# Two layers of cross attention with feed-forward: key loads, residual loads and a bias addition at other places in their queues

## The chip, the cores and the metric

One NeuronCore of one Trainium2 chip. Times are device microseconds of one execution of the whole program. One execution was also taken by the hardware profiler; all rows below are from it. TensorE (PE) does the matrix products, VectorE (DVE), ScalarE (ACT) and GpSimd (POOL) the rest; SyncE (SP) issues almost all DMA transfers, in one queue and in program order (SPq in the rows).

## The reference, cut to what matters

```
x: (32, 256, 256), context: (32, 77, 192), 16 heads of 64
x = x + attention0(layernorm(x), context)       # Wq, Wk, Wv, Wo, bo; softmax over 77 keys
x = x + down(silu(gate(n)) * up(n))             # n = layernorm(x); 256 -> 768 -> 256, int weights / 127
x = x + attention1(layernorm(x), context)       # same shapes, other weights
x = x + dequantised(int8(n) @ int8(rhs))        # n = layernorm(x); row and column scales absmax / 127
```

## The kernel before, in words

A first stage turns the context into keys and values of both layers, as high and low 16-bit halves, and stores them in DRAM. The main stage runs 64 batches: `h` = 0 to 31 are the 32 batches of layer 0, `h` = 32 to 63 those of layer 1. Each engine has its own `body(h, like, lay, plan)`, and the order of its work in it is written out by hand. `lay[d]` is the layer (0, 1 or None) of the batch `h + d`; work of up to seven neighbouring batches is interleaved in one body. The bodies of `h` = 4 to 28 and 36 to 60 run as hardware loops, the others are unrolled (line 815).

A body has four slots, `u` = 0 to 3, one for each unit of four heads. In slot `u`:

- TensorE computes the scores of unit `u` of batch `h` in two halves of 128 queries (line 960), queries of a unit two further on (970), the output projection of unit `u` of batch `h-1` (983) and the weighting of values three units back (998). Feed-forward products of batches `h-2` and `h-3` (1006, 1013), or the quantised product (1019), stand in between.
- VectorE takes the row maxima of the scores (1291), forms low halves (1217, 1220) and reciprocals of the denominators (1296); ScalarE computes the exponentials (1140). In slot 3 VectorE sums the projection and the residual rows `x_res` to `x1` (1399). In slot 0 of the next body follow its moments (1231, 1233).
- GpSimd makes the probabilities of a half of a unit in three operations: multiplication by the reciprocals (1436), high half (1440), low half (1442). In slot `u` it does the second half of unit `u-1`, then the first half of unit `u`. At the end of slot 3 it takes the power for the normalisation (1415, tile `rs`). At the end of slot 0 it adds the output bias to the residual rows (1465).
- SyncE turns the probabilities by a transposing DMA, one for each half of unit `u-1` in slot `u` (849, tile `pT`). The buffer `p16` exists twice: GpSimd's high half of a unit waits until the unit two before has been turned. Around the turnings stand the other transfers: residual rows in slot 0 (897), keys of units 2 and 3 in slot 0 and of units 0 and 1 of the next batch in slot 2 (833, two DMAs each, tile `kb`), values in slots 1 and 3 (840), normalised rows of layer 1 in slot 2 (907), results (913, 919, 930).

The keys of units 2 and 3 are read from slot 2 on; those of units 0 and 1, loaded in slot 2, from slot 0 of the next body. A key buffer may be overwritten once the scores that read it are done (semaphore `s_s`). The normalised rows of the next but one batch are turned by TensorE in slot 1 of the next body. The bias waits for the residual load (`s_xr`); line 1399 waits for the bias (`s_xb`).

Of the kernel before, what the change touches and what calls it, by code (L numbers as in the profile page):

```python
# [50 lines left out]
def xattn_ffn_kernel(nc, x, ctx, wq0, wk0, wv0, wo0, bo0, w_gate, w_up, w_down,  # L51
                     wq1, wk1, wv1, wo1, bo1, rhs, out):
    B, NQ, D = x.shape
# [3 lines left out]
    QT = NQ // P  # L57
# [19 lines left out]
    with stack:  # L77
# [29 lines left out]
        x_in, xn = (x_pair[:, i, :].rearrange("p (t d) -> p t d", d=D) for i in range(2))  # L107
        st1 = sb("st1", [P, QT, 6], F32)
        mv1 = sb("mv1", [P, QT, 2], F32)
        ve1 = sb("ve1", [P, QT], F32)  # L110
        rs1 = sb("rs1", [P, QT], F32)
# [535 lines left out]
        x_res = sb("x_res", [P, QT, D], F32)  # L647
# [52 lines left out]
        s_xr, s_xb, s_x1 = sem("s_xr"), sem("s_xb"), sem("s_x1")  # L700
        s_nl, s_ngo, s_ygo = sem("s_nl"), sem("s_ngo"), sem("s_ygo")
# [30 lines left out]
        def batch_of(ap, b):  # L732
            return ap[bass.ds(b, 1)].rearrange("o p t d -> (o p) t d")

        def after(eng, s, count):

            if not (isinstance(count, int) and count <= 0):
                eng.wait_ge(s, count)
# [88 lines left out]
        with nc.Block() as block:  # L827

            @block.sync
            def _(sp):  # L830
                def load_keys(g, at, l):
                    for a in range(2):
                        sp.dma_start(kb[g][a * DH:(a + 1) * DH, :, :, a * NK:(a + 1) * NK].rearrange(  # L833
                            "p r m k -> p (r m) k"),
                            keys_d[l][a * DH:(a + 1) * DH, g, :, bass.ds(at, NK)]).then_inc(s_kb[g], 16)

                def load_values(g, at, l):
                    src = vals_d[l].rearrange("r k c -> k r c")[bass.ds(at, NK), :,
                                                               g * 2 * HPU * DH:(g + 1) * 2 * HPU * DH]
                    sp.dma_start(vb[g][:, :, :], src).then_inc(s_vb[g], 16)  # L840

                def turn_probabilities(k, v, t):

                    if t == 0:
                        after(sp, s_pv, k - 3)
                        sp.sem_inc(s_pgo, 1)
                    sp.wait_ge(s_pl, QT * k + t + 1)
                    sp.sem_inc(s_pgo, 1)
                    sp.dma_start_transpose(pT[v][:, :, t * P:(t + 1) * P],  # L849
                                           p16[v % 2][:, t, :, :, :].rearrange("p r h k -> p (r h k)")).then_inc(  # L850
                                               s_pt[v], 16)

                def ready(e):

                    return e if isinstance(e, int) else sp.snap(e)

                def load_late():
                    for k, item in enumerate(late_items):
                        d, src = late_raw[:, k, :], item[0]
                        if len(src.shape) == 3:  # L860
                            d = d.rearrange("p (t d) -> p t d", d=D)
                        sp.dma_start(d, src).then_inc(s_late, 16)

                sp.sem_inc(s_y, 16)
                sp.sem_inc(s_ys, 16)
                sp.wait_ge(s_xn, QT)
                sp.dma_start(x_in[:, :, :], batch_of(x_src[0], 1)).then_inc(s_x, 16)
                sp.wait_ge(s_kz, 4)
                load_keys(0, 0, 0)
                load_keys(1, 0, 0)  # L870
                sp.wait_ge(s_xn, QT * 2)
                sp.dma_start(x_in[:, :, :], batch_of(x_src[0], 2)).then_inc(s_x, 16)

                def body(h, like, lay, plan):
                    n = UNITS * h
                    if lay[-3] == 0:
                        b_mid = ready(h - 3)
                    if lay[-2] == 1:
                        b_out = ready(h - 2 - B)
                    if lay[-1] is not None:  # L880
                        b_res = ready(h - 1 - lay[-1] * B)
                    if lay[0] is not None:
                        at_own = ready((h - lay[0] * B) * NK)
                    if lay[1] is not None:
                        at_next = ready((h + 1 - lay[1] * B) * NK)
                    if lay[2] == 1:
                        b_far = ready(h + 2 - B)
                    if lay[3] == 0:
                        b_first = ready(h + 3)
                    for u in range(UNITS):  # L890
                        turning = lay[(u - 1) // UNITS] is not None
                        if u == 0 and lay[-1] is not None:
                            after(sp, s_x1, h - 1)
                            if lay[-1] == 1:
                                sp.sem_inc(s_ngo, 1)
                                sp.wait_ge(s_y, 16 * (h - 1 - B + 2))
                            sp.dma_start(x_res[:, :, :], batch_of(x_src[lay[-1]], b_res)).then_inc(s_xr, 16)
                        if turning:
                            turn_probabilities(n + u - 1, (u - 1) % UNITS, 0)
                        if u == 1 and lay[0] is not None:  # L900
                            after(sp, s_pv, n - 2)
                            load_values(0, at_own, lay[0])
                        if u == 2 and lay[2] == 1:
                            sp.wait_ge(s_ys, 16 * (h + 4 - B))
                            sp.sem_inc(s_ngo, 1)
                            sp.wait_ge(s_xt, h + 2)
                            sp.dma_start(xn, batch_of(n_rows, b_far)).then_inc(s_nl, 16)
                        if u == 2 and lay[1] is not None:
                            sp.wait_ge(s_s, QT * (n + 2))
                            load_keys(0, at_next, lay[1])  # L910
                        if u == 3 and lay[-2] == 1:
                            sp.wait_ge(s_ysum, h - 1 - B)
                            sp.dma_start(batch_of(out_rows, b_out), yo[:, :, :]).then_inc(s_yo, 16)
                        if u == 3 and lay[0] is not None:
                            after(sp, s_pv, n)
                            load_values(1, at_own, lay[0])
                        if u == 3 and lay[-3] == 0:
                            sp.wait_ge(s_yn, QT * (h - 2))
                            sp.dma_start(batch_of(n_rows, b_mid), yn[:, :, :]).then_inc(s_ys, 16)
                        if turning:  # L920
                            turn_probabilities(n + u - 1, (u - 1) % UNITS, 1)
                        if u == 3 and lay[3] == 0:
                            sp.wait_ge(s_xn, QT * (h + 3))
                            sp.dma_start(x_in[:, :, :], batch_of(x_src[0], b_first)).then_inc(s_x, 16)
                        if u == 0 and lay[0] is not None and like > 0:
                            sp.wait_ge(s_s, QT * n)
                            load_keys(1, at_own, lay[0])
                        if u == 2 and lay[-3] == 0:
                            sp.wait_ge(s_yd, QT * (h - 2))
                            sp.dma_start(batch_of(mid_rows, b_mid), y[:, :, :]).then_inc(s_y, 16)  # L930
                        if like == 0 and u == 3:
                            load_late()

                bodies(sp, body)
                sp.wait_ge(s_y, 16 * (B + 1))
                sp.wait_ge(s_ys, 16 * (B + 1))
                sp.wait_ge(s_yo, 16 * B)
# [474 lines left out]
            def _(pool):  # L1412
                def inverse(k, ve, rs, count):
                    pool.wait_ge(s_var[k], count)
                    pool.tensor_tensor(rs[:, :], ve[:, :], half_neg[:, :], ALU.pow).then_inc(s_inv[k], 1)  # L1415
# [7 lines left out]
                def body(h, like, lay, plan):  # L1423
# [21 lines left out]
                    for u in range(UNITS):  # L1445
# [13 lines left out]
                            pool.tensor_copy(y[:, :, :], x1[:, :, :]).then_inc(s_yx, 1)  # L1459
                        if lay[0] is not None:  # L1460
                            probabilities(h, u, 0)
                        if u == 0 and lay[-1] is not None:
                            pool.wait_ge(s_xr, 16 * h)
                            bias = bo_b[lay[-1]][:, :].unsqueeze(1).to_broadcast([P, QT, D])
                            pool.tensor_tensor(x_res[:, :, :], x_res[:, :, :], bias, ALU.add).then_inc(s_xb, 1)
                        if u == 1 and lay[2] == 0:
                            inverse(0, ve1, rs1, h + 2)
                        if u == 2 and lay[-2] == 0:
                            low_hidden(0, h - 2)
                        if u == 2 and lay[-3] == 0:  # L1470
# [32 lines left out]
```

## Time and profile before

| | |
|---|---|
| median of 3 runs | 1768.03 us |
| all runs | 1763.06, 1768.2, 1768.03 us |
| the profiled execution | 1763.16 us, its span 1761.4 us |
| granted TensorE clock, mean | 0.988 |
| busy share of the span | PE 93%, ACT 78%, DVE 77%, POOL 72% |
| hardware DMA queue | 282.87 MB, 74.0% of the 16 DMA engines' time |

The page gives the busy share of every engine over the whole span. The stages differ, so the rows below are taken from stretches of it: layer 0 runs to about 1070 us, the turnover to about 1170, layer 1 from there to about 1730. In a row of the timeline the columns are the start, the time busy, engine, line, operation, what it writes and reads, and in brackets the idle time before it and what ended it. In the waits the columns are the total in us, the number of waits and the longest.

### The profile page before, as it was taken

How to read it: one execution, taken by the hardware profiler on the slowest of the kernel's cores; microseconds unless marked ns; L12 is line 12 of the kernel's file. 1: busy time of each engine (PE TensorE's matmuls, PEld its weight loads, DVE VectorE, ACT ScalarE, POOL GpSimd, SP SyncE). 2: the span in 40 equal slices, each digit the busy share in tenths (PEclk: the TensorE clock that was granted, in tenths of full speed). 3: DMA queues.
4: the chain of work that ended last, by engine and by line, in shares of the span. 5: the costliest groups of instructions: out<-in, count | busy, mean ns of one | idle time of the engine just before them, and what ended most of it. 6: DMA issues, size and time to landing. Idle time of an engine off the chain costs nothing.

```text
span 1761.4 us, 56617 instructions
## 1 busy us (share of the span) xinstructions
PE 1646.6 (93%) x16300; PEld 1399.7 (79%) x16300; DVE 1359.9 (77%) x3471; ACT 1373.6 (78%) x5650; POOL 1268.4 (72%) x1920
## 2 busy tenths in 40 slices
PE   7999858999999999999999999999989999899995
PEld 6888746888888888888888888877777777777773
DVE  5666646888888888888888887787777777777775
ACT  5555548888888888888888887788888888888883
POOL 3000157878888888887888887888888888888883
PEclk9999989999999999999999999999999999999998
DMA  8666757776666667666666677798888888888894
GB/s 234 223 227 221 253 140 152 138 149 144 139 147 147 136 148 149 135 149 149 136 148 151 129 148 154 133 186 175 174 174 174 173 177 177 171 174 173 178 177 85
DMA packets 807766, 288.45 MB, mean 164 GB/s; under 512 B 686000, under 2 KB 795472, under 8 KB 807696
## 3 DMA queue, kind: packets, MB, share of 16 engines
q1 hardware_dynamic: 806432, 282.87, 74.0%
q0 software_dynamic: 1264, 4.72, 0.9%
q8 instruction: 35, 0.57, 0.1%
q14 instruction: 35, 0.29, 0.1%
HBM read 87.72 MB, written 65.54 MB: 87 GB/s over the span
## 4 chain that ended last, share of the span: by engine, by line
PE 55%; SPq 8%; POOL 8%; issue 7%; DMA 3%; DVE 3%; ACT 1%; POOLq 0%; ACTq 0%; DVEq 0%
PE psum L970 12%; PE psum L983 12%; PE psum L1006 9%; PE psum L960 8%; PE psum L998 7%; SPq L849 5%; PE psum L1013 5%; POOL pr L1436 3%; DMA kb<-keys 3%; POOL p L1442 2%; POOL p L1440 2%; PE psum L946 2%; SPq L833 2%; DVE oT_l L1217 1%; ACT ex L1140 1%
## 5 line engine op out<-in xcount | busy, mean ns | idle before, releaser
L1140 ACT ACTIVATE ex<-psum,nmax 128x77 f32<-128x77 f32 x2048 | 635.5, 331 | 70.1 <-DVE nmax L1291 66.2
L1140 ACT ACTIVATION_READ_ACCUMULATOR ex<-psum,nmax 128x1 f32 x2048 | 434.7, 212 | 0.0
L1442 POOL TENSOR_TENSOR p<-pr,p 128x308 f16<-128x308 f32 x512 | 393.9, 769 | 40.9
L1436 POOL TENSOR_TENSOR pr<-ex,rden 128x308 f32<-128x308 f32 x512 | 358.8, 701 | 43.3 <-DVE rden L1296 39.8
L1291 DVE TENSOR_REDUCE nmax<-psum 128x4 f32<-128x308 f32 x512 | 240.1, 469 | 169.7 <-PE psum L960 166.1
L1440 POOL CAST p<-pr 128x308 f16<-128x308 f32 x512 | 231.4, 452 | 106.1 <-POOL pr L1436 102.6
L983 PE MATMUL psum<-wo_h,oT_h 128*128 128x256 f16 x1024 | 281.1, 275 | 24.2 <-DVE oT_l L1217 23.7
L960 PE MATMUL psum<-kb,qT_h 128*128 128x154 f16 x2048 | 257.8, 231 | 48.1 <-DMA kb<-keys 34.9
L970 PE MATMUL psum<-xT_h,wq_h 128*128 128x256 f16 x1024 | 281.1, 274 | 1.4 <-DVE xT_l L1217 1.4
L970 PE MATMUL psum<-xT_l,wq_h 128*128 128x256 f16 x1024 | 281.2, 275 | 0.0
L970 PE MATMUL psum<-xT_h,wq_l 128*128 128x256 f16 x1024 | 281.0, 274 | 0.0
L983 PE MATMUL psum<-wo_l,oT_h 128*128 128x256 f16 x1024 | 280.9, 274 | 0.0
L983 PE MATMUL psum<-wo_h,oT_l 128*128 128x256 f16 x1024 | 280.9, 274 | 0.0
L960 PEld LDWEIGHTS psum<-kb,qT_h 128*128 128x128 f16 x2048 | 167.1, 98 | 103.5 <-ACT ex L1140 45.4
L960 PE MATMUL psum<-kb,qT_l 128*128 128x154 f16 x1024 | 221.4, 230 | 0.0
L998 PE MATMUL psum<-pT,vb 77*64 77x256 f16 x3072 | 217.4, 277 | 0.0
L1102 ACT ACTIVATE oT_h<-psum 128x512 f16<-128x512 f32 x256 | 154.7, 604 | 60.8 <-PE psum L998 60.6
L998 PEld LDWEIGHTS psum<-pT,vb 77*64 77x64 f16 x3072 | 148.4, 110 | 54.6 <-issue 54.3
L1217 DVE TENSOR_TENSOR oT_l<-psum,oT_h 128x512 f16<-128x512 f32 x256 | 174.9, 683 | 14.4 <-ACT oT_h L1102 14.2
L1220 DVE SCALAR_TENSOR_TENSOR qT_l<-psum,qT_h 128x512 f16<-128x512 f32 x256 | 173.9, 679 | 0.2 <-ACT qT_h L1102 0.2
L1102 ACT ACTIVATE qT_h<-psum 128x512 f16<-128x512 f32 x256 | 156.0, 610 | 3.6 <-PE psum L970 3.6
L1415 POOL TENSOR_TENSOR rs<-ve,half_neg 128x2 f32<-128x2 f32 x127 | 88.6, 697 | 73.1 <-DVE ve L1233 70.1
(161 smaller groups left out, 3855.3 us busy)
## 6 DMA issues: line engine op xcount, KB each, us to landing
keys<-ks SPq DMA_DIRECT2D x14, 1408.0 KB, 6.3
kb<-keys SPq DMA_DIRECT2D x256, 77.0 KB, 3.2
vb<-vals SPq DMA_DIRECT2D x128, 154.0 KB
vals<-vs SPq DMA_DIRECT2D x56, 256.0 KB, 2.5
x_pair<-in_x_dram SPq DMA_DIRECT2D x32, 256.0 KB, 2.8
pT<-p SPq DMA_TRANSPOSE x512, 3.2
x_res<-in_x_dram SPq DMA_DIRECT2D x32, 256.0 KB, 3.3
mid_x<-y SPq DMA_DIRECT2D x32, 256.0 KB, 2.5
```

What stands on the lines that cost most here:

```text
L960: last = pe.matmul(o, w[:, a, ts], kb[u // 2][:, part, u % 2 * PPU + a, :], start=(q == 0), stop=(q == 2))
L970: last = pe.matmul(o[:, a, :], ww[:, k, w], xx[:, k, :], start=(q == 0), stop=(q == len(terms) - 1))
L983: last = pe.matmul(OA[:, t, :], oo[:, a, ts], ww[:, m, :], start=first, stop=(u == UNITS - 1 and a == PPU - 1 and q == 2), skip_group_chec ...
L998: last = pe.matmul(OV[b * DH:(b + 1) * DH, a, :], vb[u // 2][:, part, c:c + DH], pT[u][0:NK, pp * HPU + hd, :], start=(q == 0), stop=(q == 2))
L1102: return act.activation(dst, src, ACT.Copy, scale=scale)
L1140: last = act.activation(ex[i][:, t, b, :], SC[:, t, b * NK:(b + 1) * NK], ACT.Exp, bias=nmax[i][:, t, b:b + 1], accum_out=den[i][:, t, b:b ...
L1217: return dve.tensor_tensor(dst, src, hi, ALU.subtract)
L1220: return dve.scalar_tensor_tensor(out=qT_l[i][:, :, :], in0=src, scalar=Q_DOWN, in1=qT_h[i][:, :, :], op0=ALU.mult, op1=ALU.subtract)
L1291: dve.tensor_reduce(nmax[i][:, t, :], SC[:, t, :].rearrange("p (h k) -> p h k", k=NK), AX_X, ALU.max, negate=True).then_inc(s_m, 1)
L1436: pool.tensor_tensor(pr[:, t, :, :], ex[i][:, t, :, :], r, ALU.mult).then_inc(s_p, 1)
L1440: pool.tensor_copy(d[:, t, 0, :, 0:NK], pr[:, t, :, :]).then_inc(s_ph, 1)
L1442: pool.tensor_tensor(d[:, t, 1, :, 0:NK], pr[:, t, :, :], d[:, t, 0, :, 0:NK], ALU.subtract).then_inc(s_pl, 1)
```

## The change

On SyncE, the key loads come first in slots 0 and 2, with the same semaphore waits. The residual load (slot 0) and the load of the normalised rows (slot 2) come after both turnings of their slot. On GpSimd, the bias addition goes from the end of slot 0 to the end of slot 1, behind the power operation `inverse(0, ...)` of layer 0. No instruction is added or taken away.

```diff
                     for u in range(UNITS):
                         turning = lay[(u - 1) // UNITS] is not None
-                        if u == 0 and lay[-1] is not None:
-                            after(sp, s_x1, h - 1)
-                            if lay[-1] == 1:
-                                sp.sem_inc(s_ngo, 1)
-                                sp.wait_ge(s_y, 16 * (h - 1 - B + 2))
-                            sp.dma_start(x_res[:, :, :], batch_of(x_src[lay[-1]], b_res)).then_inc(s_xr, 16)
+                        if u == 0 and lay[0] is not None and like > 0:
+                            sp.wait_ge(s_s, QT * n)
+                            load_keys(1, at_own, lay[0])
+                        if u == 2 and lay[1] is not None:
+                            sp.wait_ge(s_s, QT * (n + 2))
+                            load_keys(0, at_next, lay[1])
                         if turning:
                             turn_probabilities(n + u - 1, (u - 1) % UNITS, 0)
...
-                        if u == 2 and lay[2] == 1:
-                            sp.wait_ge(s_ys, 16 * (h + 4 - B))
-                            sp.sem_inc(s_ngo, 1)
-                            sp.wait_ge(s_xt, h + 2)
-                            sp.dma_start(xn, batch_of(n_rows, b_far)).then_inc(s_nl, 16)
-                        if u == 2 and lay[1] is not None:
-                            sp.wait_ge(s_s, QT * (n + 2))
-                            load_keys(0, at_next, lay[1])
...
                         if turning:
                             turn_probabilities(n + u - 1, (u - 1) % UNITS, 1)
+                        if u == 0 and lay[-1] is not None:
+                            after(sp, s_x1, h - 1)
+                            if lay[-1] == 1:
+                                sp.sem_inc(s_ngo, 1)
+                                sp.wait_ge(s_y, 16 * (h - 1 - B + 2))
+                            sp.dma_start(x_res[:, :, :], batch_of(x_src[lay[-1]], b_res)).then_inc(s_xr, 16)
+                        if u == 2 and lay[2] == 1:
+                            sp.wait_ge(s_ys, 16 * (h + 4 - B))
+                            sp.sem_inc(s_ngo, 1)
+                            sp.wait_ge(s_xt, h + 2)
+                            sp.dma_start(xn, batch_of(n_rows, b_far)).then_inc(s_nl, 16)
...
-                        if u == 0 and lay[0] is not None and like > 0:
-                            sp.wait_ge(s_s, QT * n)
-                            load_keys(1, at_own, lay[0])
...
-                        if u == 0 and lay[-1] is not None:
+                        if u == 1 and lay[2] == 0:
+                            inverse(0, ve1, rs1, h + 2)
+                        if u == 1 and lay[-1] is not None:
                             pool.wait_ge(s_xr, 16 * h)
                             bias = bo_b[lay[-1]][:, :].unsqueeze(1).to_broadcast([P, QT, D])
                             pool.tensor_tensor(x_res[:, :, :], x_res[:, :, :], bias, ALU.add).then_inc(s_xb, 1)
-                        if u == 1 and lay[2] == 0:
-                            inverse(0, ve1, rs1, h + 2)
```

## Rows read from the trace of the kernel before

**Rows 1.** Busy time by stretch; first column the stretch, second its length.
```profile
core 0: us, PE busy (x) PEld busy (x) DVE busy (x) ACT busy (x) POOL busy (x), PEclk, DMA share, GB/s
1190.51:1653.69 463.18, 426.31 (x4686) 358.27 (x4683) 355.60 (x922) 390.61 (x1772) 397.13 (x598) 1.00 0.86 175
355.00:994.00 639.00, 637.43 (x6641) 548.18 (x6638) 552.34 (x1487) 537.70 (x2243) 521.22 (x803) 1.00 0.68 145
...
1096.66:1123.56 26.90, 26.00 (x276) 22.52 (x273) 20.14 (x56) 21.18 (x91) 20.89 (x32) 1.00 0.82 142
```

**Rows 2.** Waits of TensorE, GpSimd and SyncE, 1320 to 1640 us.
```profile
PE psum L960 <- DMA kb<-keys: 20.3, 15, 1.6
...
POOL pr L1436 <- DVE rden L1296: 5.7, 23, 0.3
POOL p L1440 <- DMA pT<-p: 1.5, 6, 0.3
...
SPq L848 <- POOL p L1442: 9.9, 21, 0.6
```

**Rows 3.** Groups of instructions, same stretch: busy us, mean ns | idle before.
```profile
L1415 POOL TENSOR_TENSOR rs<-ve,half_neg 128x2 f32<-128x2 f32 x16 | 11.2, 699 | 1.6
```

**Rows 4.** The chain that ended last, 1380 to 1440 us: start, us, what.
```profile
1416.46 3.10 DMA kb<-keys
```

**Rows 5.** Timeline of SyncE, one batch of layer 1.
```profile
1405.46 2.79 SPq L849 DMA_TRANSPOSE pT<-p  x2
...
1411.81 0.40 SPq L897 DMA_DIRECT2D x_res<-mid_x  x1
1412.57 2.71 SPq L849 DMA_TRANSPOSE pT<-p  x2
1415.56 1.51 SPq L833 DMA_DIRECT2D kb<-keys  x2
```

**Rows 6.** Timeline of TensorE, slot 2 of the same batch.
```profile
1419.79 0.30 PE L960 MATMUL psum<-kb,qT_h 128*128 128x154 f16 x2 [1.50 <-DMA kb<-keys]
```

**Rows 7.** DMA issues, 1391 to 1431 us; last column us to landing.
```profile
x_res<-mid_x SPq DMA_DIRECT2D x2, 256.0 KB, 2.8
```

**Rows 8.** Timeline of GpSimd, same batch.
```profile
1410.49 0.70 POOL L1415 TENSOR_TENSOR rs<-ve,half_neg 128x2 f32<-128x2 f32 x1
...
1412.73 0.75 POOL L1442 TENSOR_TENSOR p<-pr,p 128x308 f16<-128x308 f32 x1
...
1414.85 1.04 POOL L1442 TENSOR_TENSOR p<-pr,p 128x308 f16<-128x308 f32 x1
1415.86 1.26 POOL L1465 TENSOR_TENSOR x_res<-x_res,bo_b 128x512 f32<-128x512 f32 x1
1417.09 0.69 POOL L1436 TENSOR_TENSOR pr<-ex,rden 128x308 f32<-128x308 f32 x1
...
1421.64 0.70 POOL L1436 TENSOR_TENSOR pr<-ex,rden 128x308 f32<-128x308 f32 x1 [0.27 <-DVE rden L1296]
```

**Rows 9.** Timeline of VectorE, same batch.
```profile
1414.85 0.43 DVE L1331 TENSOR_SCALAR q_i<-q_a 128x512 f16<-128x512 f32 x1 [0.51 <-ACT q_a L1197]
...
1415.85 0.17 DVE L1296 RECIPROCAL rden<-den 128x4 f32<-128x4 f32 x1
...
1421.39 0.17 DVE L1296 RECIPROCAL rden<-den 128x4 f32<-128x4 f32 x1
```

**Rows 10.** The bias additions, whole span: ns min/median/max.
```profile
L1465 POOL TENSOR_TENSOR x_res<-x_res,bo_b x64: 1257/1272/1534, 268.0 to 1734.7; 128x512 f32<-128x512 f32 x64
```

**Rows 11.** Timeline of TensorE, two batches of the turnover.
```profile
1081.53 0.29 PE L960 MATMUL psum<-kb,qT_h 128*128 128x154 f16 x2 [0.92 <-issue]
...
1108.43 0.29 PE L960 MATMUL psum<-kb,qT_h 128*128 128x154 f16 x2 [0.90 <-issue]
```

**Rows 12.** DMA issues, 1076 to 1077.6 us; last column us to landing.
```profile
kb<-keys SPq DMA_DIRECT2D x2, 77.0 KB, 3.9
```

**Rows 13.** Timelines of GpSimd and VectorE, a late batch.
```profile
1692.78 0.70 POOL L1415 TENSOR_TENSOR rs<-ve,half_neg 128x2 f32<-128x2 f32 x1
...
1699.11 0.70 POOL L1436 TENSOR_TENSOR pr<-ex,rden 128x308 f32<-128x308 f32 x1
...
1698.56 0.17 DVE L1296 RECIPROCAL rden<-den 128x4 f32<-128x4 f32 x1
```

**Rows 14.** Timeline of GpSimd, one batch of layer 0.
```profile
705.00 0.69 POOL L1415 TENSOR_TENSOR rs<-ve,half_neg 128x2 f32<-128x2 f32 x1 [1.80 <-DVE ve L1233]
```

## The prediction

> **What bounds the kernel now.** I read the busy time by stage first, because the batches of the two layers are different work [rows 1]. In layer 0 TensorE is busy 637.43 of 639.00 us: nothing outside it can show in the time there. In layer 1, from 1190.51 to 1653.69 us, it is busy 426.31 of 463.18. The residual loads, one a batch, divide that stretch into 23 batches of 20.14 us; TensorE works 18.5 of them and is idle 1.6. So only layer 1 and the few batches around the turnover can answer.
>
> Second, the waits of layer 1, over 320 us or 15.9 batches [rows 2]. TensorE waits 20.3 us for key loads, 1.28 a batch, the wait that the change is about. GpSimd, only fourth in busy time on the page, waits for almost nothing: 5.7 us for reciprocals (0.36 a batch) and 1.5 us for turned probabilities (0.09), and 1.6 us stand idle ahead of its power operation (0.10) [rows 3]. Everything else in its 20.14 us is its own work and the fixed gaps between its dependent operations. The DMA-issuing queue, SyncE, waits 9.9 us for probabilities (0.62 a batch): it too is nearly full. Third, the chain of waits goes from SyncE through a key load's landing [rows 4] into TensorE's scores, on through the residual sum and its moments to GpSimd, and from GpSimd's probabilities back to SyncE. The key load is on that loop; GpSimd and SyncE are right behind it. That limits the gain: if TensorE's 1.28 us went, the batch would shrink by no more than GpSimd's own slack, 0.36 + 0.09 + 0.10 = 0.55 us.
>
> **Keys of units 2 and 3, to the head of slot 0.** Now SyncE issues in slot 0 the residual load at 1411.81, both turnings from 1412.57, and the keys from 1415.56 [rows 5]. The second half lands 3.10 us after 1416.46 [rows 4], at 1419.56, and TensorE goes on at 1419.79 after 1.50 us of idleness [rows 6]. With the keys in the place of the residual load they are issued 3.75 us earlier and land at about 1415.8. TensorE wants them at 1419.79 - 1.50 = 1418.3: 2.5 us of cover, so the wait goes. Their semaphore condition, all scores of the batch before, holds long before, since GpSimd's last probabilities, for which the turnings wait, come after those scores. What becomes late is the rest of the slot. The two key issues take 1.51 us, the residual load's place was 0.76 (1412.57 - 1411.81), so the turnings shift by 0.75 us at worst, if SyncE is then still as far behind as now. I expect them unshifted, because of the next edit.
>
> **Keys of units 0 and 1, to the head of slot 2.** Now the normalised rows and then these keys stand between the two turnings of the slot, and the second turning, at 1405.46 [rows 5], is the one whose landing GpSimd waits for [rows 2]. The keys are read a whole pair of slots later, so they gain nothing themselves. But ahead of the turnings they fill the time in which SyncE waits for GpSimd, and the second turning stands behind nothing. Gain: the 0.09 us a batch, and a SyncE that comes to slot 0 on time.
>
> **Normalised rows, behind the turnings of slot 2.** Read by TensorE in slot 1 of the next batch, three slots later; nothing is lost. **Residual load, behind the turnings of slot 0.** The turnings end their issue at 1412.57 + 2.71 = 1415.28 [rows 5], at worst 0.75 later, and the load lands 2.8 us after its issue [rows 7], so at 1418.2 to 1419.0. Its reader is the bias.
>
> **The bias, one slot later on GpSimd.** This is the part that costs. Count from the power operation at 1410.49 [rows 8]. GpSimd reaches the second half of unit 0's probabilities (the multiplication by the reciprocals, at 1417.09) 6.60 us after it, with the bias in between. Start to start the bias takes 1417.09 - 1415.86 = 1.23 us; without it GpSimd would be there after 5.37 us. But the reciprocals that this step reads are made by VectorE at 1415.85 and end at 1416.02 [rows 9], which is 5.53 us after the same power operation, and a GpSimd step follows a reciprocal by 0.08 us (1421.39 + 0.17 = 1421.56, start at 1421.64) [rows 8, 9]. The 5.53 us are a chain: power, shift, normalisation on ScalarE, row maximum, scale, the rounding for the quantised product (1414.85, VectorE waiting 0.51 us for ScalarE [rows 9]), low half of the output, reciprocal. None of it waits for keys, so it does not shorten when they come early. GpSimd would stand 5.61 - 5.37 = 0.24 us in each batch. Before, the bias covered exactly this. The later place costs nothing else. Two steps take (1421.64 - 0.27 - 1417.09) = 4.28 us [rows 8], so the bias starts 5.61 + 4.28 = 9.9 us after the power operation, at 1420.4, at least 1.4 us after its load has landed; its result is read in slot 3. It also stands ahead of the step that now waits 0.27 us for reciprocals at 1421.64, and those come earlier once the scores of unit 2 do, so the 0.36 us goes.
>
> The bias could gain or lose in length. It takes 1257 to 1534 ns, median 1272 [rows 10], so the bounds are -0.01 and +0.26 us; I take 0, by the median. The Trainium skill (SBUF — State Buffer, Who interferes with whom) says that a VectorE operation with two SBUF inputs, or in a two-port mode, and a GpSimd operation that reads SBUF exclude each other. The trace agrees: the subtraction beside the rounding at 1414.85 took 1.04 us, the others 0.75 [rows 8, 9]. By that rule the moved bias would pay only if it met such an operation; the VectorE work beside 1420.4 is a maximum and a difference that reads PSUM.
>
> **Sum for layer 1.** Gone: 0.36 + 0.09. Added: 0.24. The 0.10 ahead of the power operation goes if VectorE comes earlier with TensorE; bounds 0 and 0.10. That is 0.21 to 0.31 us a batch; I take 0.25, a batch of 19.89. Twenty-five batches run in this form (the 23 of rows 1 and one at either side): 25 x 0.25 = 6.3 us.
>
> **Turnover.** Two batches in which TensorE still does layer 0's FFN are bound by TensorE (26.00 of 26.90 us busy [rows 1]), and it stands some 0.9 us in each, just ahead of unit 2's scores [rows 11]. The profile names no releaser there, but those keys took 3.9 us to land [rows 12] in place of 3.1. I count these as key waits: 1.8 us, bounds 0 and 1.8.
>
> **Tail.** In the last batches the same count gives GpSimd 1699.11 - 1692.78 = 6.33 us with the bias, 5.10 without its 1.23, against reciprocals 1698.56 + 0.17 - 1692.78 = 5.95 us after the power operation [rows 13]. GpSimd waits for nothing there now, so the change can only lose: 0 to 0.9 us in each of two batches. I take 0.4 each, -0.8.
>
> **Layer 0.** Cost nothing. TensorE covers all: GpSimd there waits 1.80 us for VectorE once a batch [rows 14], more than the bias is long. If that cover were gone, 26 batches at 0.24 would be 6 us. The start I leave at nothing, within the 1.3 us of one bias.
>
> Sum: 6.3 + 1.8 - 0.8 = 7.3 us. The profiled execution took 1763.16 us (span 1761.4), so it would become 1755.9. The median of the runs, 1768.03, lies 4.87 above the profiled one, since two of three runs are near 1768: 1760.7, rounded to **1760**.
>
> **Rivals.**
> (a) GpSimd never waits: the chain behind the power operation is hidden after all, because VectorE and ScalarE run ahead once keys are early. Then each batch gains 0.55: 25 x 0.55 + 1.8 - 0.8 = 14.8 us, 1753. For it: GpSimd's pure work is the floor. Against: the chain starts on GpSimd itself, so running ahead does not help.
> (b) The wait is replaced in full: SyncE (0.62 us of slack) or ScalarE's exponentials hold TensorE as long as the keys did, or the keys are no earlier because SyncE comes late to the slot. Only the turnover gains, 1 to 2 us: 1766. For it: GpSimd and SyncE are within a microsecond of the period. Against: 3.75 us of lead is 2.5 times the wait.
> (c) Slower: the residual load is late. The bias wants it at 1420.4, with 1.4 to 2.2 us in hand; the load stands behind two turnings, on DMA engines that are 86% busy in this stage [rows 1]. It decides once the landing takes over 4.2 us (median 2.8), if the turnings are shifted. At 5.1 us GpSimd, which has no slack left, stands 0.9 us a batch: 25 x (0.9 - 0.25) = 16 us, less the turnover's 1: 1783. For it: key loads took 3.9 us in the turnover [rows 12]. Against: in the steady stage the load takes two thirds of that.
>
> **How the numbers follow.** Forecast 50%, (a) 20%, (b) 20%, (c) 8%, the rest 2%. The forecast's own range is 1756 to 1764: terms of 0.21 to 0.31 a batch, 0 to 1.8, 0 to -1.8, and 2.5 us for which of the two times of the runs the median falls on. With (a) in and most of (b): 1750 to 1767. A difference under 0.3%, 5.3 us, can't be told from none. Faster (under 1762.7): most of the forecast and all of (a), 0.71. Same: most of (b) and the upper end of the forecast, 0.22. Slower: 0.07.
>
> **What would show it.** Right: TensorE has no wait for keys in layer 1; the batch is 19.8 to 20.0 us; GpSimd waits some 0.2 us for reciprocals in every batch, now ahead of the second half of unit 0 and no more in slots 2 and 3; none for turned probabilities; layer 0 stays at 26.2 us. Wrong: a batch of 19.6 (rival a) or 20.1 (b), or a GpSimd wait for the residual load (c).

## The result, and the profile after

| | before | after |
|---|---|---|
| median of 12 runs each | 1768.12 us | 1774.1 us |
| lowest to highest | 1761.77 to 1772.81 | 1771.85 to 1782.97 |
| profiled execution, span | 1763.16, 1761.4 us | 1771.97, 1770.2 us |

The ratio is 1.0042, 95% interval 1.0027 to 1.0058. The change made the kernel slower, where 1760 us was forecast.

One sum per batch, VectorE's `x1` (line 1399), divides both traces in the same way. The start of each of those operations gives this ledger:

| stretch | before | after | difference |
|---|---|---|---|
| start of the span to batch 1 | 281.97 | 285.25 | +3.28 |
| batches 2 to 28 (layer 0) | 709.13 | 704.86 | -4.27 |
| batches 29 to 35 (turnover) | 174.76 | 172.24 | -2.52 |
| batches 36 to 60 (layer 1) | 504.11 | 514.03 | +9.92 |
| batches 61 to 64 | 78.57 | 80.97 | +2.40 |

The first row is not put down to the change. The context stage runs without the edited code, and 2.33 of the 3.28 us are there already at the first row maximum of the main stage (236.97 us before, 239.30 after). The first `x1` lay between 285.29 and 288.56 us in every other profiled execution below, with the bias and the keys in either place. Without this row, 5.5 of the 8.8 us between the two profiled executions are left; the medians differ by 6.0. In the settled part a layer 0 batch went from 26.22 to 26.09 us, one of layer 1 from 20.14 to 20.57.

The stretches of the kernel after that answer to [rows 1] (stretch, length, busy time by engine, clock, DMA share, GB/s):

```profile
1182.79:1676.38 493.59, 453.69 (x4898) 373.61 (x4898) 382.96 (x960) 402.22 (x1849) 409.05 (x625) 1.00 0.84 171
355.00:994.00 639.00, 637.40 (x6666) 550.74 (x6664) 536.25 (x1495) 537.15 (x2255) 519.22 (x808) 1.00 0.67 145
```

The waits of the kernel after, 1320 to 1640 us, 15.6 batches, for [rows 2]:

```profile
PE psum L960 <- DVE qT_l L1220: 14.9, 15, 1.0
...
POOL pr L1436 <- DVE rden L1296: 18.4, 15, 1.2
...
SPq L848 <- POOL p L1442: 16.7, 16, 1.1
...
DVE nmr L1238 <- POOL rs L1415: 23.3, 16, 1.5
```

TensorE's wait for keys is gone, as is GpSimd's for turned probabilities, and SyncE, which had 0.62 us of slack a batch, now has 1.07. All that the change set out to do on SyncE it did. GpSimd's wait for reciprocals has grown from 5.7 to 18.4 us. It is now one wait a batch of 1.22 us, at the place that the prediction named, where 0.24 us was forecast. These are GpSimd and VectorE of one batch after, for [rows 8, 9]:

```profile
1433.54 0.70 POOL L1415 TENSOR_TENSOR rs<-ve,half_neg 128x2 f32<-128x2 f32 x1
1434.19 0.71 POOL L1436 TENSOR_TENSOR pr<-ex,rden 128x308 f32<-128x308 f32 x1
...
1439.77 0.70 POOL L1436 TENSOR_TENSOR pr<-ex,rden 128x308 f32<-128x308 f32 x1 [1.23 <-DVE rden L1296]
```
```profile
1434.27 0.65 DVE L1238 SCALAR_TENSOR_TENSOR nmr<-mv,rs 128x2 f32<-128x2 f32 x1 [1.45 <-POOL rs L1415]
...
1438.45 0.43 DVE L1331 TENSOR_SCALAR q_i<-q_a 128x512 f16<-128x512 f32 x1 [0.72 <-ACT q_a L1197]
1438.83 0.69 DVE L1217 TENSOR_TENSOR oT_l<-psum,oT_h 128x512 f16<-128x512 f32 x1
1439.44 0.17 DVE L1296 RECIPROCAL rden<-den 128x4 f32<-128x4 f32 x1
```

The chain from the power operation at 1433.54 to the step at 1439.77 takes 6.23 us; 5.61 were forecast from [rows 8, 9]. The new part stands at its head. The shift (`nmr`, two numbers a partition) takes 0.65 us. It starts 0.08 us after GpSimd has begun to multiply, and ends within 0.02 us of that multiplication. In the trace of before it took 0.16 (with the reciprocals that the multiplication reads):

```profile
1410.92 0.16 DVE L1296 RECIPROCAL rden<-den 128x4 f32<-128x4 f32 x1
1411.22 0.16 DVE L1238 SCALAR_TENSOR_TENSOR nmr<-mv,rs 128x2 f32<-128x2 f32 x1
```

It started there 0.73 us after the power operation, as it does now (1434.27 - 1433.54). But GpSimd's multiplication came 0.78 us after that operation, and now comes 0.65 after it. The reciprocals that it reads ended 0.59 us after the start of the power operation; now they end 0.73 us ahead of it, and the multiplication starts before the shift. The order was a matter of 0.1 us already in the kernel before. In its batches with power operations at 1672.58 and 1692.78 the multiplication started 0.67 us after the power operation, and the shift took 0.66 us:

```profile
1673.31 0.66 DVE L1238 SCALAR_TENSOR_TENSOR nmr<-mv,rs 128x2 f32<-128x2 f32 x1
```

What put the multiplication at 0.78 us in the other batches, with reciprocals that ended at 0.59 us in both, is not shown.

The chain is 0.62 us longer than forecast, and the shift makes 0.49 of that. The rest is two small pieces: VectorE's scale (line 1284) takes 0.30 us where it took 0.24, and GpSimd starts 0.16 us behind the end of the reciprocals, not 0.08. GpSimd's own way to that step became shorter, 5.01 us where 5.37 was forecast: its multiplication starts 0.1 us sooner, and its low half (1442) takes 0.75 us in place of 1.04, now that VectorE's rounding starts only near its end. So 0.24 us became 0.24 + 0.62 + 0.36 = 1.22. The last term lengthens the wait and not the batch.

The chain of waits of the kernel after, same view as [rows 4], runs through exactly these steps and no more through SyncE or a key load (start, us, what; three pieces named "issue" left out behind the shift and the row maximum):

```profile
1433.54 0.71 POOL rs L1415
1434.27 0.06 DVE nmr L1238
...
1434.84 0.48 DVE nmax L1291
...
1435.46 0.59 ACT x L1106
1436.08 0.70 DVE am L1379
...
1438.45 0.44 DVE q_i L1331
...
1439.77 0.71 POOL pr L1436
```

### The profile page after: what moved, and what is told of

It reads as the page before. It is cut to its first block, busy times and chain, and to the rows that moved or that the text cites. A ratio compares the mean times of both kernels' runs of the same rounds, so it can differ in the third digit from the quotient of the medians.

```text
span 1770.2 us, 56617 instructions
## 1 busy us (share of the span) xinstructions
PE 1652.9 (93%) x16300; PEld 1400.5 (79%) x16300; DVE 1351.7 (76%) x3471; ACT 1364.7 (77%) x5650; POOL 1254.7 (71%) x1920
## 4 chain that ended last, share of the span: by engine, by line
PE 46%; POOL 19%; issue 11%; DVE 5%; ACT 3%; DMA 1%; POOLq 1%; SPq 0%; ACTq 0%; DVEq 0%
PE psum L970 9%; PE psum L1006 9%; PE psum L983 9%; POOL pr L1436 7%; PE psum L960 6%; PE psum L998 5%; POOL p L1440 5%; PE psum L1013 5%; POOL p L1442 2%; POOL x_res L1467 2%; PE psum L946 2%; POOL rs L1415 1%; DVE am L1379 1%; ACT q_a L1197 1%; ACT x L1106 1%
## 5 line engine op out<-in xcount | busy, mean ns | idle before, releaser
L1140 ACT ACTIVATION_READ_ACCUMULATOR ex<-psum,nmax 128x1 f32 x2048 | 457.4, 223 | 0.0
L983 PEld LDWEIGHTS psum<-wo_h,oT_h 128*128 128x128 f16 x1024 | 100.3, 98 | 53.4 <-DVE oT_l L1217 37.2
```

The costliest lines, as they stand in the source:

```text
L983: last = pe.matmul(OA[:, t, :], oo[:, a, ts], ww[:, m, :], start=first, stop=(u == UNITS - 1 and a == PPU - 1 and q == 2), skip_group_chec ...
L1140: last = act.activation(ex[i][:, t, b, :], SC[:, t, b * NK:(b + 1) * NK], ACT.Exp, bias=nmax[i][:, t, b:b + 1], accum_out=den[i][:, t, b:b ...
```

## The experiments

The first four ran in one set (before: 1771.06 us, median of 24 runs), the last three in another (1770.33, 11 runs). The changed kernel was not timed again in them, so what is said against it goes by the ratios to before and by the batch lengths in the traces. Theory A in all: the loss comes from the bias leaving the place where it covered the chain behind the power operation, and the key order by itself is a gain.

**Keys alone.** The bias stays at the end of slot 0, so the residual load stays first.

```diff
 # the changed kernel, with
+ (SyncE, slot 0) residual load ahead of load_keys(1, ...), no more behind the turnings
- (GpSimd) if u == 1 and lay[-1] is not None: bias
+ (GpSimd) if u == 0 and lay[-1] is not None: bias
```

> Keys first in slots 0 and 2 as in the change, but the bias stays at the end of slot 0, so the residual load stays first in slot 0 (the keys right behind it). Theory A (the loss comes from the bias leaving its place, where it covered the chain from GpSimd's power operation to the reciprocals of unit 0's second half): GpSimd needs 5.01 + 1.23 us from the power operation to that step, the chain 6.23, so no wait; a layer 1 batch of 19.35 to 19.5 us, against 20.14 before and 20.57 after. Layer 0 stays at 26.22. In all about 1749 us where before is 1768. Rival B (the new order on SyncE or on the DMA engines is what costs, by later turnings): batch 20.4 or more, 1772 or more, the wait of some 1.2 us at that step still there.

Measured: 1751.83 us, ratio 0.9897 (0.9869 to 0.9924). A layer 1 batch takes 19.70 us, one of layer 0 26.22. GpSimd waits for nobody in layer 1; its only listed idle time is the fixed gap ahead of its own cast:

```profile
POOL p L1440 <- POOL pr L1436: 27.0, 130, 0.3
```

Rival B is out. The batch is 0.2 to 0.35 us longer than I expected. GpSimd's own operations are longer here, 1502 ns for the bias and 761 for a multiplication, where the changed kernel has 1268 and 699; its low halves are a little shorter, 754 ns against 792 (groups of instructions, keys-only kernel):

```profile
L1436 POOL TENSOR_TENSOR pr<-ex,rden 128x308 f32<-128x308 f32 x131 | 99.7, 761 | 0.0
...
L1465 POOL TENSOR_TENSOR x_res<-x_res,bo_b 128x512 f32<-128x512 f32 x16 | 24.0, 1502 | 0.0
```

The shift takes 0.65 us here too, so the lengthened chain is there, and covered. The bias stands over its end:

```profile
1407.20 0.70 POOL L1415 TENSOR_TENSOR rs<-ve,half_neg 128x2 f32<-128x2 f32 x1
...
1412.18 1.50 POOL L1465 TENSOR_TENSOR x_res<-x_res,bo_b 128x512 f32<-128x512 f32 x1
1413.63 0.70 POOL L1436 TENSOR_TENSOR pr<-ex,rden 128x308 f32<-128x308 f32 x1
```
```profile
1413.12 0.17 DVE L1296 RECIPROCAL rden<-den 128x4 f32<-128x4 f32 x1
```

The reciprocals end at 1413.29, while GpSimd is still adding.

**Bias alone.**

```diff
 # the kernel before, with
-                        if u == 0 and lay[-1] is not None:
-                            (bias)
                         if u == 1 and lay[2] == 0:
                             inverse(0, ve1, rs1, h + 2)
+                        if u == 1 and lay[-1] is not None:
+                            (bias)
```

> Only the bias moves to the end of slot 1; SyncE's order is that of before. Theory A: the key wait of TensorE stays, GpSimd gets a wait of 0.24 us or more at the second half of unit 0; batch 20.14 to 20.3. Layer 0 goes to 26.09, because GpSimd's low half of the hidden rows in slot 1 no longer stands behind the bias and the down product stops waiting 0.13 us: 28 x 0.13 = 3.6 us gained. In all 1764 to 1769. Rival B: the bias is harmless, batch 20.14, 1764, layer 0 as said. Rival C (layer 0's 0.13 us comes from the key order): layer 0 at 26.22.

Measured: 1781.75 us, ratio 1.0065 (1.004 to 1.0091). Layer 0 came out as expected, 26.09. Layer 1 did not: 20.56 to 20.88 a batch, not 20.14 to 20.3. Its waits, 1320 to 1640 us:

```profile
POOL pr L1436 <- DVE rden L1296: 19.6, 16, 1.2
...
PE psum L960 <- DMA kb<-keys: 1.1, 3, 0.4
```

GpSimd waits 1.23 us with the old key order too, and the shift takes 0.65 us. So the longer chain needs no early keys. The keys-only kernel shows that it needs no waiting GpSimd either: there GpSimd waits for nobody, and the shift takes 0.65 us. What all these kernels share is that the reciprocals for the multiplication behind the power operation are ready in time: they end 0.7 us ahead of its start in the changed kernel and in most batches here, 0.1 us ahead with the keys alone, and 0.59 us after it in the kernel before. The key wait of TensorE has all but gone although the keys stand where they stood in SyncE's order. TensorE is held by others now: 15.6 us by VectorE's low halves of the queries (1220) and 5.6 us by exponentials (1140). Why its batches are up to 0.3 us longer than those of the changed kernel was not followed up.

**GpSimd waits for the shift.**

```diff
                         if u == 3 and lay[-1] is not None:
                             inverse(1, ve2, rs2, h)
+                            if lay[-1] == 1:
+                                pool.wait_ge(s_nmr[1], h)
```

> The changed kernel, with one wait more: in layer 1 GpSimd, after the power operation, waits until VectorE has made the shift from it, before it multiplies again. Theory A says that the shift takes 0.65 us in place of 0.16 because GpSimd's multiplication starts 0.08 us before it and both read SBUF through one port: then the shift is back at 0.16, the chain at about 5.75 in place of 6.23, the batch at 14.34 + 5.75 = 20.1, total about 1763. Rival D (the length of the shift is not what lengthens the chain, the wait only delays GpSimd): batch 20.57 or up to 0.3 more, total 1774 to 1781.

Measured: 1766.69 us, ratio 0.9983 (0.9967 to 0.9999), 20.20 a batch. In its trace the 16 shifts of the stretch took (ns min/median/max)

```profile
L1238 DVE SCALAR_TENSOR_TENSOR nmr<-mv,rs x16: 160/161/161, 1329.8 to 1632.8; 128x2 f32<-128x2 f32 x16
```

and in the changed kernel

```profile
L1238 DVE SCALAR_TENSOR_TENSOR nmr<-mv,rs x16: 648/648/648, 1331.4 to 1639.9; 128x2 f32<-128x2 f32 x16
```

One wait more makes the kernel 0.37 us a batch faster. Rival D is out: the 0.49 us is the overlap with GpSimd's multiplication and it does lengthen the batch. The reciprocals of unit 0's second half end 5.46 us after the power operation (1415.16 + 0.17 - 1409.87), in place of 6.07. The wait costs GpSimd 0.72 us a batch in its place, and its own way to unit 0's second half then takes 5.81 us, so that it no longer waits there for the reciprocals (last row, VectorE):

```profile
1409.87 0.70 POOL L1415 TENSOR_TENSOR rs<-ve,half_neg 128x2 f32<-128x2 f32 x1
1411.29 0.70 POOL L1436 TENSOR_TENSOR pr<-ex,rden 128x308 f32<-128x308 f32 x1 [0.72 <-DVE nmr L1238]
...
1415.68 0.70 POOL L1436 TENSOR_TENSOR pr<-ex,rden 128x308 f32<-128x308 f32 x1
```
```profile
1415.16 0.17 DVE L1296 RECIPROCAL rden<-den 128x4 f32<-128x4 f32 x1
```

The Trainium skill (SBUF — State Buffer, Who interferes with whom) has this case: a VectorE instruction with two SBUF inputs contends with a GpSimd instruction that reads SBUF, and issue order decides who blocks. The shift reads `mv` and `rs`, both in SBUF; by that rule it waits for the rest of the multiplication, and the 0.65 us agrees.

**Reciprocals ahead of the rounding.** In layer 1, VectorE makes the reciprocals of unit 0's second half before it rounds for the quantised product.

```diff
+                        if u == 1 and lay[-2] == 1 and lay[0] is not None:
+                            reciprocals(n, 0, 1)
                         if u == 1 and lay[-2] == 1:
                             dve.wait_ge(s_qa, QT * (h - 1 - B))
                             (rounding)
 ...
-                        if lay[(u - 1) // UNITS] is not None:
+                        if lay[(u - 1) // UNITS] is not None and not (u == 1 and lay[-2] == 1):
                             reciprocals(n + u - 1, (u - 1) % 2, 1)
```

> The changed kernel, with VectorE's reciprocals of unit 0's second half moved ahead of the rounding for the quantised product (layer 1 only). Their input is ready when ScalarE has done the exponentials, about 4.3 us after the power operation (3.3 before, 0.5 later by the longer shift, with the reciprocals 0.4 after that), and GpSimd is there after 5.01. Theory A: GpSimd waits no more; batch 14.34 + 5.01 = 19.35, up to 19.6; total about 1747. Rival B (turnings or SyncE hold the batch): batch 20.4 to 20.6, total 1773, GpSimd waiting somewhere else.

Measured: 1768.57 us, ratio 0.9986 (0.9969 to 1.0003), 20.31 a batch. The wait at that step is gone, as expected. The gain, 0.26 us a batch, was about a quarter of what I expected, because the same chain goes on through VectorE to the reciprocals of unit 1's first half, the next that GpSimd needs:

```profile
1413.38 0.70 POOL L1417 TENSOR_TENSOR rs<-ve,half_neg 128x2 f32<-128x2 f32 x1
...
1418.36 0.93 POOL L1438 TENSOR_TENSOR pr<-ex,rden 128x308 f32<-128x308 f32 x1
...
1421.45 0.70 POOL L1438 TENSOR_TENSOR pr<-ex,rden 128x308 f32<-128x308 f32 x1 [0.70 <-DVE rden L1296]
```

It is still GpSimd's wait for VectorE and no turning; rival B is out here too. I had taken the first late operand for the only one. Both lie behind the chain, and a bias at the end of slot 0 covers both.

**Bias by layer.** The keys-only kernel, with the bias at the end of slot 1 where layer 0's rows are added.

```diff
-                        if u == 0 and lay[-1] is not None:
+                        if u == 0 and lay[-1] == 1:
                             (bias)
                         if u == 1 and lay[2] == 0:
                             inverse(0, ve1, rs1, h + 2)
+                        if u == 1 and lay[-1] == 0:
+                            (bias)
```

> The keys-only kernel, with the bias at the end of slot 1 in batches that add layer 0's residual rows and at the end of slot 0 in those of layer 1. Theory A: both gains together: layer 0 at 26.09 us a batch (the down product no longer waits 0.13 us), layer 1 at 19.70. About 28 x 0.13 = 3.6 us below the keys-only kernel's 1751.8: 1748. Rival: the layer 0 gain belongs to the key order and the bias together, or is lost at the turnover: 1752.

Measured: 1749.12 us, ratio 0.988 (0.9862 to 0.9898): 26.09 us a batch in layer 0 and 19.68 to 19.71 in the settled part of layer 1. Its profiled execution is 4.5 us shorter than the keys-only one. Between the medians of the two the difference, 2.7 us, is near what the runs scatter. It has the lowest time of all kernels here.

**Slot 0 keys alone.** The kernel before with `load_keys(1, ...)` moved up behind the residual load, and nothing else.

```diff
                             sp.dma_start(x_res[:, :, :], batch_of(x_src[lay[-1]], b_res)).then_inc(s_xr, 16)
+                        if u == 0 and lay[0] is not None and like > 0:
+                            sp.wait_ge(s_s, QT * n)
+                            load_keys(1, at_own, lay[0])
```

> The kernel before with one edit: the keys of units 2 and 3 go to slot 0 right behind the residual load, ahead of both turnings; the keys of units 0 and 1 and the normalised rows stay between the turnings of slot 2. Theory A (the key wait of TensorE was the outermost of the limits, GpSimd the next): batch 19.7, no key wait, total 1752, perhaps 0.1 us a batch more for GpSimd's wait for turned probabilities, 1754. Rival (the reorder of slot 2 carried the gain, by letting SyncE catch up): batch 20.0 or more, 1763 to 1768.

Measured: 1756.8 us, ratio 0.9925 (0.9908 to 0.9942), 19.71 a batch. The one edit carries the gain of the key order. The edit of slot 2 adds what it was reckoned at, GpSimd's wait for turned probabilities (2.1 us in 320, 0.13 a batch), but in the settled batches this does not show in the length. The two profiled executions are level up to batch 60 (1660.21 and 1660.46 us); 2.9 of the 3.2 us between them arise in the last four. I did not follow these up.

**Bias back, SyncE as changed.** This asks whether the two edits had to go together.

```diff
 # the changed kernel, with
-                        if u == 1 and lay[-1] is not None:
+                        if u == 0 and lay[-1] is not None:
                             (bias)
```

> The changed kernel with SyncE's whole new order, but the bias back at the end of slot 0, so that it follows its load closely. The load would be issued about 4.4 us after the power operation (second turning's probabilities 2.9, issue 1.3, gap 0.2) and land 2.8 to 3.2 later, at 7.2 to 7.6; GpSimd wants it at 5.0. Theory A: GpSimd waits 2.2 to 2.6 us for the residual load in each layer 1 batch; batch 19.7 + 2.4 = 22.1, total 1752 + 28 x 2.4 = about 1815, layer 0 at 26.22 or more. Rival: the load is not late; batch 19.7, 1752.

Measured: 1862.45 us, ratio 1.0529 (1.0509 to 1.055), batches of 21.2 to 25.3 us in layer 1, 23.4 on average.

```profile
1411.10 0.70 POOL L1415 TENSOR_TENSOR rs<-ve,half_neg 128x2 f32<-128x2 f32 x1
...
1420.38 1.27 POOL L1465 TENSOR_TENSOR x_res<-x_res,bo_b 128x512 f32<-128x512 f32 x1 [4.26 <-DMA x_res<-mid_x]
```
```profile
1412.17 1.50 SPq L833 DMA_DIRECT2D kb<-keys  x2
1414.05 2.68 SPq L849 DMA_TRANSPOSE pT<-p  x2
1417.17 0.41 SPq L919 DMA_DIRECT2D x_res<-mid_x  x1
```

Behind the turnings the residual load goes out 6.1 us after the power operation, not 4.4, since the keys push the turnings back, and lands at 9.3. The mechanism was right, the size 4.0 us a batch (55.7 us in 14 waits) in place of 2.4. One thing more differs here: in layer 1 the granted TensorE clock of this kernel was 0.94, where the changed kernel's was 1.00 over the same stretch (the third figure from the end of each row, this kernel first). From 1410 to 1420 us, for one, with TensorE busy for 6.88 us, it was 0.83, so part of that stretch ran at the lower of the two levels, 1.2 and not 2.4 GHz. How much of the length is the clock was not separated.

```profile
1200.00:1700.00 500.00, 425.07 (x4330) 350.66 (x4328) 341.29 (x854) 358.73 (x1640) 364.34 (x554) 0.94 0.73 150
1200.00:1700.00 500.00, 460.03 (x4968) 379.02 (x4966) 388.60 (x976) 408.12 (x1876) 414.91 (x634) 1.00 0.85 171
```

So a residual load behind the turnings forces the bias out of slot 0, and the bias out of slot 0 is the loss. The key loads need neither: the 0.76 us of issue that the residual load takes ahead of them is no burden on keys with 2.5 us of cover.

## Why the prediction was wrong, step by step

- **Keys of units 2 and 3.** Right: the wait is gone in all kernels that issue these keys ahead of the turnings, but for 2.8 us in four waits where the bias went back. Rival (a), the 0.55 us a batch that it can give, is nearly what the keys alone gave: 20.14 to 19.70, 0.44.
- **Keys of units 0 and 1, normalised rows.** Right: they took GpSimd's 0.09 us away and cost nothing.
- **Residual load.** Right in the settled batches: no wait for it there in the changed kernel, and rival (c) did not happen. In the last batch GpSimd did wait for it:

```profile
1748.14 1.26 POOL L1467 TENSOR_TENSOR x_res<-x_res,bo_b 128x512 f32<-128x512 f32 x1 [4.21 <-DMA x_res<-mid_x]
```

  No loss can be seen from it. The last `x1` follows the one before by 21.12 us, and by 21.36 with the keys alone, where nothing waits for that load.
- **The bias: the step that failed.** The place and the mechanism were right, and the term was mis-sized. A batch is GpSimd's way from unit 0's second half round to the power operation, plus the chain from there. The first part was reckoned at 19.89 - 5.61 = 14.28 us and measured 1433.54 - 1419.20 = 14.34. The chain was put at 5.61, carried over from before, and measured 6.23 (14.34 + 6.23 = 20.57, the batch). "So it does not shorten when they come early" was true and not enough: it got longer. 0.49 of the 0.62 us is the shift behind the multiplication; keeping the two apart gave 0.37 us a batch back (third experiment), GpSimd's own way then being the longer. The longer chain stood in the prediction's own rows: in the late batch of [rows 13] the reciprocals end 5.95 us after the power operation, where [rows 8, 9] give 5.53, and the shift of that batch took 0.66 us. I used the 5.95 for the tail and did not ask why it was longer. I weighed the port rule for the moved bias alone, and not for the operations that the new wait shifts against each other. 25 x (0.25 + 0.43) = 17 us is more than the whole miss of 14; layer 0 gave some of it back.
- **Turnover.** Forecast 1.8 us, measured 2.5. The waits there were key waits: they are gone in the changed kernel and with the keys alone, and with the bias alone two of them, 0.57 and 0.93 us, are left. The seven batches take 172.01 us with the keys alone and 174.98 with the bias alone.
- **Tail.** Forecast -0.8, measured -2.4. The cause of layer 1 is at work here too: GpSimd waits 2.4 us for reciprocals in three waits over the last 92 us, 0.7 before, and not at all with the keys alone, which lose 0.2 there. It need not be the only one, since the kernel with slot 0 keys alone loses 3.1 us in these batches and has the bias in its old place. That is open.
- **Layer 0, "cost nothing".** Wrong, for the better: 0.13 us a batch. TensorE was busy without a gap in both, but the first down product of a batch took 1.44 us in the chain of before and 1.31 after:

```profile
714.98 1.44 PE psum L1013 x12
```
```profile
715.41 1.31 PE psum L1013 x12
```

  It comes with the bias (bias alone 26.09, keys alone 26.22). The expectation of the second experiment gave GpSimd's low half of the hidden rows (1426) as the reason, and the trace does not bear that out: in the kernel before it ends at 713.30, 1.62 us ahead of the product's first weight load. What ends 0.12 us ahead of that load is VectorE's low half of the normalised rows (`xT_l`, at 714.80), which frees the bank that the product writes:

```profile
714.11 0.69 DVE L1217 TENSOR_TENSOR xT_l<-psum,xT_h 128x512 f16<-128x512 f32 x1
714.92 0.10 PEld L1013 LDWEIGHTS psum<-wdT,hT_h 128*128 128x128 f16 x1
```

  VectorE was late there because of the bias. Its own low half of the hidden rows, which reads two operands in SBUF, started 0.02 us behind GpSimd's bias addition and took 1.53 us. With the bias elsewhere it took 0.41 (before, before, after):

```profile
711.22 1.27 POOL L1465 TENSOR_TENSOR x_res<-x_res,bo_b 128x512 f32<-128x512 f32 x1
711.24 1.53 DVE L1217 TENSOR_TENSOR hT_l<-hf,hT_h 128x256 f16<-128x256 f32 x1
```
```profile
711.66 0.41 DVE L1217 TENSOR_TENSOR hT_l<-hf,hT_h 128x256 f16<-128x256 f32 x1
```

  It takes 1.53 us also with the keys alone, and 0.41 also with the bias alone and with the bias by layer. So the same kind of overlap that cost the shift 0.49 us in layer 1 was what the moved bias took away in layer 0. A wait of 0.13 us did not show as idle time of TensorE but as a longer first product.
- **The chances.** The forecast counted a loss only where a load would be late (8%). A loss by GpSimd's order, with no load late at all, had no share.

## What to carry to other kernels

An operation that nobody waits for may be covering a wait. Before it is moved, list on its engine which operand each later step needs, and when that operand is made; if the step would come first, the chain behind that operand becomes the period. Then its length must be worked out anew, because engines that change their lead over one another change who blocks whom: a wait of 0.24 us on paper became 1.22. Where two rows give two lengths for the same chain, as 5.53 and 5.95 us did here, find out why before one of them is used. And when a change bundles several moves, look for the one that forces the others. Here one moved pair of key loads gave 0.75% by itself.

## What the hardware showed that I had not expected

A VectorE operation on two numbers a partition takes 0.16 us or 0.65 us, to the nanosecond the same in all 16 batches (160 to 161, or 648), by whether it starts 0.05 us before or 0.08 us after a GpSimd multiplication that reads SBUF (0.16 also where that multiplication was held back). Making GpSimd wait for it cost GpSimd 0.72 us and still shortened each batch by 0.37 us. In layer 0 a VectorE subtraction took 1.53 us behind GpSimd's bias addition and 0.41 without it.
